# First self attention, units that begin with their scores: all maxima, projections and turned rows behind them

## The chip, the core and the metric

The kernel runs on one core of a Trainium2 chip. The metric is the device time of one execution in microseconds. Before the change it is 1828.26 us (median of 3 runs, 1827.87 to 1830.49).

## The reference

Two decoder blocks work one after the other on x (2 batches, 1024 tokens, width 256). Each has a self attention, a cross attention to 77 context rows, and a feed-forward layer, with a layer norm before each. The change touches only the first block's self attention, with 16 heads of width 64 and no mask:

```
h = _layernorm(x, ln1_g, ln1_b)
q = (xq @ wq).reshape(B, S, N_HEADS, D_HEAD)      # k, v alike
attn = jnp.einsum('bihd,bjhd->bhij', q, k) * scale
attn = jax.nn.softmax(attn, axis=-1)
out = jnp.einsum('bhij,bjhd->bihd', attn, v).reshape(B, S, D_ATTN)
x = out @ wo + bo + x
```

## The kernel before

The function `wide_attention` computes this attention. A **block** is one group g of 2 heads for one batch b; there are 16 (8 groups times 2 batches), written by `both(g, b)`. A block has 8 **units** u0 to u7, and a unit has two **steps**: a step is 128 keys against 512 queries for both heads, steps 0 to 7 for the first half of the queries, 8 to 15 for the second. The groups 1 to 6 run in a loop, the others are written out.

What a unit does on each engine:

- ScalarE writes ("seeds") minus the row maxima into the banks of the scores (L1243), TensorE adds the scores on them (`scores`, L1164: 3 products of high and low parts, 2 heads, so 6 matmuls a step), ScalarE takes the exponential into `sa_p_buf` (L1233), GpSimd adds up the exponentials for the denominators (L1412), TensorE multiplies the exponentials of the unit before with the values (`weighted`, L1179), two steps behind.
- Beside it stand **items** of preparation, for this block ("c"), the next ("n") or the one before ("p"), by the table `lanes`: ("k", h) and ("q", h) project keys and queries (`project`, L1110, 6 matmuls); ScalarE takes the high part out of the bank (L1226) and VectorE the rest (L1307). ("m", qt, half) are maxima: 2 matmuls, one for each head, of 128 queries against 512 keys into two banks (`maxima`, L1126), and VectorE reduces each bank to row maxima (L1325). ("t", h) turns the joined maxima (joined by VectorE at L1340, turned at L1131), VectorE copies them (L1333) and two DMAs take them through memory to all partitions (L1050, L1052). ("den", h) sums the denominators (L1138), ScalarE copies them out (L1256), VectorE inverts them (L1347).

All items share three banks, `sa_front0` to `sa_front2`, used in turn. Which bank each item has and what must have been emptied before is worked out once (`places`), and TensorE waits for it in front of an item (`wait_free`), for both banks of a maxima item before its first matmul. The scores have four banks and the weighted sums the eighth.

The order of work on TensorE is the order in which `both` writes it. `leading` gives the items of a unit up to and with its first maxima item, `trailing` the rest. In front of the scores of a unit stand the leading items, behind them the trailing ones, then the weighted sums. ScalarE, VectorE and GpSimd have their own written orders and meet TensorE at semaphores only. The table for all blocks but the first:

```
0: [("c", ("m", 5, 1)), ("c", ("m", 6, 1)), ("n", ("k", 0))],
1: [("c", ("m", 7, 1)), ("n", ("q", 0)), ("c", ("t", 1)), ("p", ("den", 1))],
2: [("n", ("m", 0, 0)), ("n", ("m", 1, 0)), ("n", ("k", 1))],
3: [("n", ("m", 2, 0)), ("n", ("m", 3, 0))],
4: [("n", ("m", 0, 1)), ("n", ("m", 1, 1)), ("n", ("q", 1))],
5: [("n", ("m", 2, 1)), ("n", ("m", 3, 1)), ("c", ("den", 0))],
6: [("n", ("t", 0)), ("n", ("m", 4, 0)), ("n", ("m", 5, 0))],
7: [("n", ("m", 6, 0)), ("n", ("m", 7, 0)), ("n", ("m", 4, 1))],
```

The first block has a table of its own (`lanes_first`) with the values' projections (L764) added. The last block has no items for a next one.

Of the kernel before, what the change touches and what calls it, by code (L numbers as in the profile page):

```python
# [51 lines left out]
def lin(g, b, per, k):  # L52

    return g * (2 * per) + (b * per + k)
# [762 lines left out]
def wide_attention(nc, name, hT, ident, ones, first_w, oT, spare, prefetch=()):  # L817
# [55 lines left out]
    def lanes_of(g, b):  # L873

        return lanes_first if isinstance(g, int) and (g, b) == (0, 0) else lanes
# [51 lines left out]
    def bank(item, k=0):  # L927
        return BODY[item, k] % NBANK

    def is_first(g, b):  # L930
        return isinstance(g, int) and (g, b) == (0, 0)

    def is_last(g, b):
        return isinstance(g, int) and (g, b) == (NG - 1, 1)
# [5 lines left out]
    def before(g, b):  # L940
        return (g, 0) if b == 1 else (g - 1, 1)
# [4 lines left out]
    def owner(who, g, b):  # L946

        if who == "c":
            return g, b
        if who == "p":  # L950
            return None if is_first(g, b) else before(g, b)
        return None if is_last(g, b) else after(g, b)

    def owned(u, g, b):

        return [(owner(who, g, b), item) for who, item in lanes_of(g, b)[u] if owner(who, g, b) is not None]

    def leading(u, g, b):

        table = lanes_of(g, b)[u]  # L960
        first = [item[0] for _, item in table].index("m") + 1
        return [x for x in owned(u, g, b) if x[1] in [item for _, item in table[:first]]]

    def trailing(u, g, b):

        return owned(u, g, b)[len(leading(u, g, b)):]

    def sums(s):

        return (KT - 1) * (s // KT) + max(s % KT, 1)  # L970
# [12 lines left out]
    with ExitStack() as ctx:  # L983
# [61 lines left out]
        with nc.Block() as block:  # L1045
# [39 lines left out]
            def _(pe):  # L1085
                def wait_free(g, b, item, *made_of):

                    at = 2 * g + b if isinstance(g, int) else 2 + b
                    counts = [DRAINED[at, part, 0] for part in made_of]
                    for k in range(2 if item[0] == "m" else 1):  # L1090
                        by, value = FREE[at, item, k]
                        if by == "den":
                            pe.wait_ge(den_taken, value if isinstance(g, int) else shifted(value, g, HALVES))
                        elif by == "front":
                            counts.append(value)
                    if counts:
                        pe.wait_ge(drained, max(counts) if isinstance(g, int) else shifted(max(counts), g, NDRAIN))

                def project(g, b, item):
                    a = 0 if item[0] == "q" else 1  # L1100
                    fr = front_ps[bank(item)]
                    if item == ("k", 0):
                        pe.wait_ge(w_split, g + 1)
                    c = b * HALVES + item[1]
                    if isinstance(g, int) and g == 0:
                        pe.wait_ge(h_low, c + 1)
                    parts = [(ws[:, a, kd, :], hs[:, kd, tokens(c)]) for kd in range(KD)
                             for ws, hs in ((w_hi, h_hi), (w_hi, h_lo), (w_lo, h_hi))]
                    for n, (ws, hs) in enumerate(parts):
                        mm = pe.matmul(fr[:], ws, hs, start=(n == 0), stop=(n == len(parts) - 1))  # L1110
                    mm.then_inc(front_full, 1)

                def values(n):
                    if n in IN_FRONT:
                        if n >= IN_FRONT.start + NSCORE:
                            pe.wait_ge(v_made, n - NSCORE + 1)
                        first_w.values(pe, n, spare_bank(n)).then_inc(v_full, 1)
                    else:
                        first_w.values(pe, n, front_ps[bank(("v", n))][:]).then_inc(front_full, 1)

                def maxima(g, b, item):
                    _, qt, half = item
                    wait_free(g, b, item, ("q", qt // QH), ("k", half))
                    for j in range(G):
                        r = slice(dh * j, dh * j + dh)
                        pe.matmul(front_ps[bank(item, j)][:], q_hi[r, b, qt * P:(qt + 1) * P],  # L1126
                                  k_hi[r, b, half * HALF:(half + 1) * HALF], start=True, stop=True).then_inc(front_full, 1)

                def turn(g, b, item):
                    pe.wait_ge(joined, lin(g, b, HALVES, item[1] + 1))  # L1130
                    pe.transpose(front_ps[bank(item)][0:G * QH, 0:P], m_row[:].rearrange("p g t -> p (g t)"),  # L1131
                                 ident[:]).then_inc(front_full, 1)

                def denominators(g, b, item):
                    h = item[1]
                    pe.wait_ge(added, lin(g, b, NADD, (KT - 1) * (h + 1)))
                    for j in range(G):
                        mm = pe.matmul(front_ps[bank(item)][64 * j:64 * j + 64, :], ones[:, 0:64], acc[:, h, j, :],  # L1138
                                       start=True, stop=True)
                    mm.then_inc(front_full, 1)  # L1140

                def front_item(g, b, item):
                    if item[0] == "m":
                        maxima(g, b, item)
                        return
                    if not (item[0] == "v" and item[1] in IN_FRONT):
                        wait_free(g, b, item)
                    if item[0] in ("q", "k"):
                        project(g, b, item)
                    elif item[0] == "v":  # L1150
                        values(item[1])
                    elif item[0] == "t":
                        turn(g, b, item)
                    else:
                        denominators(g, b, item)

                def scores(g, b, s):
                    h, kt = divmod(s, KT)
                    pe.wait_ge(seeded, lin(g, b, TILES, (s + 1) * G))
                    keys, queries = slice(kt * P, (kt + 1) * P), slice(h * HALF, (h + 1) * HALF)  # L1160
                    for part, (ks, qs) in enumerate(((k_hi, q_hi), (k_hi, q_lo), (k_lo, q_hi))):
                        for j in range(G):
                            r = slice(dh * j, dh * j + dh)
                            mm = pe.matmul(score_ps[s % len(score_ps)][:, j, :], ks[r, b, keys], qs[r, b, queries], start=False,  # L1164
                                           stop=(part == 2), skip_group_check=True)
                            if part == 2:
                                mm.then_inc(score_full, 1)
# [18 lines left out]

                def both(g, b):
                    for u in range(UNITS):
                        for of, item in leading(u, g, b):
                            front_item(*of, item)  # L1190
                        scores(g, b, 2 * u)
                        scores(g, b, 2 * u + 1)
                        for of, item in trailing(u, g, b):
                            front_item(*of, item)
                        if u >= 1:
                            weighted(g, b, 2 * u - 2)
                            weighted(g, b, 2 * u - 1)
                        elif not is_first(g, b):
                            weighted(*before(g, b), STEPS - 2)
                            weighted(*before(g, b), STEPS - 1)  # L1200
                    if is_last(g, b):
                        weighted(g, b, STEPS - 2)
                        weighted(g, b, STEPS - 1)
                        wait_free(g, b, ("den", 1))
                        pe.wait_ge(added, lin(g, b, NADD, sums(STEPS - 3)))
                        for j in range(G):
                            parts = [acc[:, 1, j, :]] + [p_buf[:, n % NPB, j, :] for n in (STEPS - 2, STEPS - 1)]
                            for n, p in enumerate(parts):
                                mm = pe.matmul(front_ps[bank(("den", 1))][64 * j:64 * j + 64, :], ones[:, 0:64], p,
                                               start=(n == 0), stop=(n == len(parts) - 1))  # L1210
                        mm.then_inc(front_full, 1)
# [1400 lines left out]
```

## Time and profile before

| | |
|---|---|
| median of 3 runs | 1828.26 us |
| profiled execution | 1825.43 us, span 1823.7 us |
| TensorE clock granted, mean | 0.98 |
| matmul busy | 1666.9 us (91%) |
| VectorE, ScalarE, GpSimd busy | 1167.3, 1067.1, 960.0 us |
| scores of the first self attention | from 74.8 to 763.8 us of the span |

The profile records one execution. PE is TensorE's matmuls, PEld its weight loads, DVE VectorE, ACT ScalarE, POOL GpSimd, SPq the queue that issues DMAs. Names starting with sa_ belong to the attention at hand; x and o are buffers lent to it. In a timeline each row is a start, a duration, an engine and what it did; a time in brackets is idle time of the engine before it and what ended it. Ends of matmuls are modelled, so starts are the better guide. In rows of TensorE "x2" are the two heads' matmuls, which start together in the two halves of the array; an fp32 product that is not split into parts is recorded as two.

### The profile page before, as it was taken

Reading aid. Unit: us, or ns where it says so; the run is one execution under the profiler, and the core shown is the slowest. Engines: PE = TensorE matmul, PEld = TensorE weight load, DVE = VectorE, ACT = ScalarE, POOL = GpSimd, SP = SyncE. Lnnn points to the kernel's source line nnn. Section 1 sums busy time; section 2 is a strip of 40 time slices with the busy share of each in tenths; the row PEclk is TensorE's granted clock in tenths of the full one; section 3 lists DMA queues with packets and bytes.
Section 4 is the critical chain, followed back from the end, with each engine's and each line's share of the span. In section 5 each row is a group of like instructions: output and inputs, shape, how many; then the busy total and the mean of one; then the engine's idle time right before and its main releaser. Section 6 shows DMA issues by size and latency. Waiting matters only on the chain. (4 is left out here: it accounts for less than half of the span.)

```text
span 1823.7 us, 28743 instructions
## 1 busy us (share of the span) xinstructions
PE 1666.9 (91%) x9636; PEld 1034.5 (57%) x9636; DVE 1167.3 (64%) x2023; ACT 1067.1 (59%) x1407; POOL 960.0 (53%) x734
## 2 busy tenths in 40 slices
PE   5889999999999999898999889996989988898799
PEld 3334444444444444386666878884544436555679
DVE  4456777767777777375776843447787845787613
ACT  4437888888888888744554433310676773444452
POOL 1237898888889888851222620201334443666205
PEclk9999999999999999999999999996999999999999
DMA  2001211101111111030000011102334321000001
GB/s 90 18 24 35 68 53 35 40 35 43 55 40 35 40 35 48 12 105 26 1 1 1 13 33 26 28 12 66 75 72 106 72 72 31 10 1 7 28 17 47
DMA packets 54210, 70.84 MB, mean 39 GB/s; under 512 B 18208, under 2 KB 41916, under 8 KB 54111
## 3 DMA queue, kind: packets, MB, share of 16 engines
q1 hardware_dynamic: 54111, 69.54, 13.5%
q8 instruction: 59, 0.97, 0.2%
q14 instruction: 40, 0.33, 0.1%
HBM read 41.72 MB, written 2.37 MB: 24 GB/s over the span
## 5 line engine op out<-in xcount | busy, mean ns | idle before, releaser
L1412 POOL TENSOR_TENSOR x<-x,sa_p_buf 128x1024 f32<-128x1024 f32 x190 | 452.5, 2382 | 107.7 <-ACT sa_p_buf L1233 95.3
L1325 DVE TENSOR_REDUCE sa_mx<-sa_front 128x1 f32<-128x512 f32 x512 | 327.3, 681 | 109.2 <-PE sa_front L1126 107.4
L1233 ACT ACTIVATE sa_p_buf<-sa_score 128x1024 f32<-128x1024 f32 x256 | 249.2, 1024 | 116.6 <-PE sa_score L1164 116.6
L1179 PE MATMUL sa_out<-sa_p_buf,sa_v_buf 128*64 128x512 f32 x1024 | 246.2, 602 | 0.0
L607 ACT ACTIVATE sa_p_buf<-sa_score 128x1024 f32<-128x1024 f32 (+1 forms) x160 | 140.6, 942 | 75.0 <-PE sa_score L555 74.8
L402 DVE TENSOR_REDUCE sa_mx<-sa_front 128x1 f32<-128x512 f32 (+1 forms) x224 | 136.5, 651 | 31.3 <-PE sa_front L316 27.6
L1987 POOL TENSOR_TENSOR x<-x,bias_out 128x1024 f32<-128x1024 f32 x24 | 60.1, 2518 | 164.5 <-POOLq L2316 142.0
L1854 POOL TENSOR_TENSOR ca_probs<-ca_s_sb,ca_inv 128x616 f32<-128x616 f32 x64 | 78.1, 1220 | 120.5 <-DVE ca_inv L1770 120.5
L1179 PEld LDWEIGHTS sa_out<-sa_p_buf,sa_v_buf 128*64 128x64 f32 x1024 | 64.9, 136 | 126.8 <-issue 99.1
L1126 PE MATMUL sa_front<-sa_k_hi,sa_q_hi 64*128 64x512 f32 x512 | 116.7, 451 | 19.1 <-DVE sa_mx L1325 15.6
L1243 ACT ACTIVATE sa_score<-sa_m_all 128x1024 f32<-128x1024 f32 x128 | 130.8, 1034 | 0.4 <-ACT o L775 0.4
L1243 ACT ACTIVATE sa_score<-x 128x1024 f32<-128x1024 f32 x128 | 127.6, 1029 | 2.3 <-DMA x<-sa_m_line 2.3
L660 POOL TENSOR_SCALAR_AFFINE_SELECT sa_p_buf<-sa_p_buf 128x128 f32<-128x128 f32 x256 | 66.0, 296 | 119.3 <-ACT sa_p_buf L607 119.3
L1347 DVE RECIPROCAL x<-x 128x128 f32<-128x128 f32 x124 | 108.7, 920 | 17.8 <-ACT x L1256 17.6
L1126 PEld LDWEIGHTS sa_front<-sa_k_hi,sa_q_hi 64*128 64x128 f32 x512 | 48.0, 183 | 124.6 <-DVE sa_mx L1325 61.4
L1164 PE MATMUL sa_score<-sa_q_hi,sa_k_hi 64*128 64x512 f32 x512 | 108.2, 419 | 2.9 <-ACT sa_score L1243 2.9
L1677 ACT ACTIVATE ca_turned<-ca_t_ps 128x1024 f32<-128x1024 f32 x64 | 65.5, 1024 | 73.7 <-PE ca_t_ps L1623 73.7
L1164 PE MATMUL sa_score<-sa_q_hi,sa_k_lo 64*128 64x512 f32 x512 | 101.1, 390 | 0.0
L1164 PE MATMUL sa_score<-sa_q_lo,sa_k_hi 64*128 64x512 f32 x512 | 100.9, 390 | 0.0
L1412 POOL TENSOR_TENSOR x<-sa_p_buf 128x1024 f32<-128x1024 f32 x32 | 76.2, 2382 | 33.9 <-ACT sa_p_buf L1233 33.9
L316 PE MATMUL sa_front<-sa_k_top,sa_q_top 33*128 33x128 f32 (+4 forms) x504 | 71.2, 348 | 22.9 <-DVE sa_mx L402 16.0
L316 PEld LDWEIGHTS sa_front<-sa_k_top,sa_q_top 33*128 33x128 f32 (+1 forms) x504 | 43.7, 193 | 77.1 <-DVE sa_mx L402 51.5
(241 smaller groups left out, 3528.6 us busy)
## 6 DMA issues: line engine op xcount, KB each, us to landing
sa_v_buf<-o SPq DMA_DIRECT2D x16, 512.0 KB, 5.1
sa_m_all<-sa_m_line SPq DMA_DIRECT2D x16, 512.0 KB, 3.7
x<-sa_m_line SPq DMA_DIRECT2D x16, 512.0 KB, 4.3
x<-in_x SPq DMA_DIRECT2D x8, 512.0 KB, 6.8
sa_q_stack<-sa_hi SPq DMA_DIRECT2D x32, 128.0 KB, 2.7
sa_k_stack<-sa_hi SPq DMA_DIRECT2D x32, 128.0 KB, 2.6
sa_recip<-sa_den_out SPq DMA_DIRECT2D x32, 128.0 KB, 2.7
ff_w<-in_L_xattn_ff_w SPq DMA_DIRECT2D x16, 128.0 KB, 2.2
```

The source lines that it names most:

```text
L316: mm = pe.matmul(bank(i, item, u)[:, c0 + lo_k:c0 + hi_k], q_top[base:base + rows_of, b, r, at], k_top[base:base + rows_of, b, r, k0 + lo_ ...
L402: dve.tensor_reduce(mx[:, b, j, place:place + 1], fr[u][:, 0:n], AX.X, ALU.max).then_inc(drained, 1)
L607: nc.scalar.activation(p_buf[:, n % NPB, 2 * r:2 * r + 2, 0:cols], score_ps[r][:, :, 0:cols], ACT.Exp, scale=SCALE).then_inc(exp_done, 1)
L1126: pe.matmul(front_ps[bank(item, j)][:], q_hi[r, b, qt * P:(qt + 1) * P], k_hi[r, b, half * HALF:(half + 1) * HALF], start=True, stop=True) ...
L1164: mm = pe.matmul(score_ps[s % len(score_ps)][:, j, :], ks[r, b, keys], qs[r, b, queries], start=False, stop=(part == 2), skip_group_check= ...
L1179: mm = pe.matmul(out_ps[64 * j:64 * j + 64, :], v_buf[:, b, kt, 64 * j:64 * j + 64], p_buf[:, s % NPB, j, :], start=(kt == 0), stop=(kt == ...
L1233: nc.scalar.activation(p_buf[:, s % NPB], score_ps[s % len(score_ps)][:], ACT.Exp, scale=SCALE).then_inc(exp_done, G)
L1243: nc.scalar.activation(score_ps[s % len(score_ps)][:], m_all[h].rearrange("p (j n) -> p j n", j=G), ACT.Identity).then_inc(seeded, G)
L1325: dve.tensor_reduce(mx[:, b, j, qt, half:half + 1], front_ps[bank(item, j)][:], AX.X, ALU.max).then_inc(drained, 1)
L1347: dve.reciprocal(recip[:, h, at], recip[:, h, at]).then_inc(inverted, 1)
L1412: nc.gpsimd.tensor_tensor(acc[:, h], prev, cur, ALU.add).then_inc(added, 1)
L1854: nc.gpsimd.tensor_tensor(probs[:, n % 2, :, 0:TC], s_sb[:, n % NS], inv[:, n % 2, :].unsqueeze(2).to_broadcast((P, U, TC)), ALU.mult).the ...
```

## The change

`leading` and `trailing` are gone. In each unit TensorE now has the scores of both steps first, and then all items of the unit in the table's order, and the weighted sums. Tables, banks, the counts waited for and the other engines' programs are as they were.

```
                 def both(g, b):
                     for u in range(UNITS):
-                        for of, item in leading(u, g, b):
-                            front_item(*of, item)
                         scores(g, b, 2 * u)
                         scores(g, b, 2 * u + 1)
-                        for of, item in trailing(u, g, b):
+                        for of, item in owned(u, g, b):
                             front_item(*of, item)
                         if u >= 1:
                             weighted(g, b, 2 * u - 2)
```

The first place is u3 of a block on TensorE. sa0_front is a bank of the items, sa0_score0 and sa0_score1 are the scores of the unit's two steps. Before:

```order
L1126 MATMUL sa0_front0<-sa0_k_hi,sa0_q_hi 128x512
L1126 MATMUL sa0_front1<-sa0_k_hi,sa0_q_hi 128x512
L1164 MATMUL sa0_score0<-sa0_q_hi,sa0_k_hi 128x512 x2
L1164 MATMUL sa0_score0<-sa0_q_lo,sa0_k_hi 128x512 x2
L1164 MATMUL sa0_score0<-sa0_q_hi,sa0_k_lo 128x512 x2
L1164 MATMUL sa0_score1<-sa0_q_hi,sa0_k_hi 128x512 x2
L1164 MATMUL sa0_score1<-sa0_q_lo,sa0_k_hi 128x512 x2
L1164 MATMUL sa0_score1<-sa0_q_hi,sa0_k_lo 128x512 x2
L1126 MATMUL sa0_front2<-sa0_k_hi,sa0_q_hi 128x512
L1126 MATMUL sa0_front0<-sa0_k_hi,sa0_q_hi 128x512
L1179 MATMUL sa0_out<-sa0_p_buf,sa0_v_buf 64x512 x4
```

The same unit now (the lines' numbers are lower by ten):

```order
L1154 MATMUL sa0_score0<-sa0_q_hi,sa0_k_hi 128x512 x2
L1154 MATMUL sa0_score0<-sa0_q_lo,sa0_k_hi 128x512 x2
L1154 MATMUL sa0_score0<-sa0_q_hi,sa0_k_lo 128x512 x2
L1154 MATMUL sa0_score1<-sa0_q_hi,sa0_k_hi 128x512 x2
L1154 MATMUL sa0_score1<-sa0_q_lo,sa0_k_hi 128x512 x2
L1154 MATMUL sa0_score1<-sa0_q_hi,sa0_k_lo 128x512 x2
L1116 MATMUL sa0_front0<-sa0_k_hi,sa0_q_hi 128x512
L1116 MATMUL sa0_front1<-sa0_k_hi,sa0_q_hi 128x512
L1116 MATMUL sa0_front2<-sa0_k_hi,sa0_q_hi 128x512
L1116 MATMUL sa0_front0<-sa0_k_hi,sa0_q_hi 128x512
L1169 MATMUL sa0_out<-sa0_p_buf,sa0_v_buf 64x512 x4
```

The six rows of scores moved ahead of the first maxima item, so the second item's use of bank 0 stands two matmuls behind the first one's.

The second place is u6 on TensorE, which has the turned row (L1131 before, L1121 now). Before:

```order
L1131 MATMUL sa0_front2<-ident,sa0_m_row 8x128
L1126 MATMUL sa0_front0<-sa0_k_hi,sa0_q_hi 128x512
L1126 MATMUL sa0_front1<-sa0_k_hi,sa0_q_hi 128x512
L1164 MATMUL sa0_score0<-sa0_q_hi,sa0_k_hi 128x512 x2
...
L1164 MATMUL sa0_score1<-sa0_q_hi,sa0_k_lo 128x512 x2
L1126 MATMUL sa0_front2<-sa0_k_hi,sa0_q_hi 128x512
L1126 MATMUL sa0_front0<-sa0_k_hi,sa0_q_hi 128x512
```

And now:

```order
L1154 MATMUL sa0_score0<-sa0_q_hi,sa0_k_hi 128x512 x2
...
L1154 MATMUL sa0_score1<-sa0_q_hi,sa0_k_lo 128x512 x2
L1121 MATMUL sa0_front2<-ident,sa0_m_row 8x128
L1116 MATMUL sa0_front0<-sa0_k_hi,sa0_q_hi 128x512
L1116 MATMUL sa0_front1<-sa0_k_hi,sa0_q_hi 128x512
L1116 MATMUL sa0_front2<-sa0_k_hi,sa0_q_hi 128x512
L1116 MATMUL sa0_front0<-sa0_k_hi,sa0_q_hi 128x512
```

The turned row moved behind the scores with the maxima that led.

## Rows read from the trace of the kernel before

**Rows 1.** Busy time by stretch: PE, PEld, DVE, ACT, POOL, granted clock, DMA
```profile
300.00:400.00 100.00, 97.66 (x545) 47.62 (x544) 74.80 (x119) 85.69 (x100) 88.22 (x42) 1.00 0.12 40
...
100.00:130.00 30.00, 25.75 (x110) 11.49 (x109) 14.99 (x26) 11.88 (x14) 10.42 (x5) 1.00 0.11 36
...
776.00:780.00 4.00, 4.00 (x10) 3.19 (x10) 2.36 (x2) 4.00 (x4) 0.00 (x0) 0.50 0.71 231
```
**Rows 2.** Timeline of TensorE, u0 and the start of u1
```profile
400.50 0.50 PE L1126 MATMUL sa_front<-sa_k_hi,sa_q_hi 64*128 64x512 f32 x2
...
400.84 0.40 PE L1164 MATMUL sa_score<-sa_q_hi,sa_k_hi 64*128 64x512 f32 x2
...
402.22 0.39 PE L1126 MATMUL sa_front<-sa_k_hi,sa_q_hi 64*128 64x512 f32 x2
402.54 0.50 PE L1110 MATMUL sa_front<-sa_h_hi,sa_w_hi 128*128 128x512 f32 x1
...
404.14 1.94 PE L1179 MATMUL sa_out<-sa_p_buf,sa_v_buf 128*64 128x512 f32 x8
406.01 0.50 PE L1126 MATMUL sa_front<-sa_k_hi,sa_q_hi 64*128 64x512 f32 x2
...
407.83 0.51 PE L1110 MATMUL sa_front<-sa_h_hi,sa_w_hi 128*128 128x512 f32 x1
```
**Rows 3.** Timeline of VectorE in u0 and u1
```profile
401.04 1.29 DVE L1325 TENSOR_REDUCE sa_mx<-sa_front 128x1 f32<-128x512 f32 x2 [1.01 <-PE sa_front L1126]
402.64 1.29 DVE L1325 TENSOR_REDUCE sa_mx<-sa_front 128x1 f32<-128x512 f32 x2 [0.32 <-PE sa_front L1126]
...
407.87 0.17 DVE L1340 TENSOR_REDUCE sa_m_row<-sa_mx 128x8 f32<-128x16 f32 x1
```
**Rows 4.** Timeline of TensorE, u7 to the next block
```profile
436.40 0.51 PE L1126 MATMUL sa_front<-sa_k_hi,sa_q_hi 64*128 64x512 f32 x2
...
438.47 0.40 PE L1126 MATMUL sa_front<-sa_k_hi,sa_q_hi 64*128 64x512 f32 x2
439.64 0.50 PE L1126 MATMUL sa_front<-sa_k_hi,sa_q_hi 64*128 64x512 f32 x2 [0.78 <-DVE sa_mx L1325]
440.07 1.94 PE L1179 MATMUL sa_out<-sa_p_buf,sa_v_buf 128*64 128x512 f32 x8
441.94 0.50 PE L1126 MATMUL sa_front<-sa_k_hi,sa_q_hi 64*128 64x512 f32 x2
```
**Rows 5.** Timeline of TensorE, first block
```profile
83.66 0.40 PE L1126 MATMUL sa_front<-sa_k_hi,sa_q_hi 64*128 64x512 f32 x2
85.42 0.50 PE L1110 MATMUL sa_front<-sa_h_hi,sa_w_hi 128*128 128x512 f32 x1 [1.37 <-DVE sa_mx L1325]
...
115.30 0.49 PE L1126 MATMUL sa_front<-sa_k_hi,sa_q_hi 64*128 64x512 f32 x2 [0.78 <-DVE sa_mx L1325]
117.17 0.50 PE L1110 MATMUL sa_front<-sa_h_hi,sa_w_hi 128*128 128x512 f32 x1 [1.38 <-DVE sa_mx L1325]
```
**Rows 6.** Timeline of TensorE, u4 and the start of u6
```profile
421.65 0.49 PE L1126 MATMUL sa_front<-sa_k_hi,sa_q_hi 64*128 64x512 f32 x2
...
424.04 0.50 PE L1110 MATMUL sa_front<-sa_h_hi,sa_w_hi 128*128 128x512 f32 x1
...
432.29 0.27 PE L1131 MATMUL sa_front<-ident,sa_m_row 128*8 128x128 f32 x1
```
**Rows 7.** Timeline of ScalarE, u0
```profile
401.83 1.94 ACT L1233 ACTIVATE sa_p_buf<-sa_score 128x1024 f32<-128x1024 f32 x2 [1.41 <-PE sa_score L1164]
...
403.65 1.03 ACT L1243 ACTIVATE sa_score<-sa_m_all 128x1024 f32<-128x1024 f32 x1
```
**Rows 8.** DMA queue, its landing (KB, us), and the seed that needs it
```profile
434.55 0.33 SPq L1052 DMA_DIRECT2D sa_m_all<-sa_m_line  x1
...
sa_m_all<-sa_m_line SPq DMA_DIRECT2D x1, 512.0 KB, 3.9
...
439.70 1.02 ACT L1243 ACTIVATE sa_score<-sa_m_all 128x1024 f32<-128x1024 f32 x1
```

More of the change, by code:

```diff
@@ L956, in owned @@
         return [(owner(who, g, b), item) for who, item in lanes_of(g, b)[u] if owner(who, g, b) is not None]
[L958 to L966, printed above, removed]
     def sums(s):
@@ L1188, in both @@
                     for u in range(UNITS):
-                        for of, item in leading(u, g, b):
-                            front_item(*of, item)
                         scores(g, b, 2 * u)
                         scores(g, b, 2 * u + 1)
-                        for of, item in trailing(u, g, b):
+                        for of, item in owned(u, g, b):
                             front_item(*of, item)
```

## The prediction

> **What bounds the kernel now.** I read the busy time by stretch first: in the first self attention TensorE is 98% busy at full clock, GpSimd 88%, ScalarE 86%, VectorE 75% [rows 1]. A busy share does not say that an engine has no holes, so I then read the timeline of one block (one group of heads of one batch; eight units u0 to u7) on TensorE. The reader is to look at the start times, not at the durations: two matmuls of one kind in the two halves of the array start as a pair, and the six pairs of a unit's scores take 402.22 - 400.84 = 1.38, 0.23 each, though each is recorded as 0.39. By start times a unit is maxima 0.34, scores 1.38, maxima 0.32, projection 1.60, weighted sums 1.87, and then the next unit's maxima, with nothing left between [rows 2]. So TensorE's program order is the path here. A block takes 441.94 - 400.50 = 41.44 us [rows 2, 4]; the first exponential after the scores starts 401.83 - 400.84 = 0.99 after them, and the seed that the next unit's scores need starts 1.82 later and takes 1.03 [rows 7], so scores could follow scores after some 3.9 us, and all units but the short ones take longer. ScalarE is ahead.
>
> Next come the three banks that maxima, projections, turned rows and sums share. One maxima item fills two of them, VectorE empties both in 1.29, and starts 0.54 after the matmuls when they come first after other work, 0.42 when matmuls of the same kind ran before [rows 2, 3]. Two maxima items need four banks. The scores between them hide this: 400.50 to 402.22 is 1.72, longer than the 1.29 in which the first bank is free again (0.54 + 0.75, see next). Where two items stand together, the second waits: 438.47 to 439.64 is 1.17, which is 0.42 and 0.75 for the first of the two reductions and the signal behind it [rows 4]. A projection behind two maxima waits for both banks: 83.66 to 85.42 is 1.76, and behind an item that itself had waited 115.30 to 117.17, 1.87 [rows 5]. These three prices are the whole prediction.
>
> **The change, part by part.** No instruction is added or removed, and only TensorE's order changes. In a full block the leading maxima go behind the scores in all units, and so the turned row in u6. ScalarE, VectorE, GpSimd and the DMA queue keep their orders. What waits behind a stalled maxima item on TensorE is the projection, the weighted sums and, through them, the next unit's scores; ScalarE's exponentials and GpSimd's additions wait for those.
>
> I sum from the start of a unit to the start of its last part (weighted sums, or the projection or sums before it), which keep their own length. Scores that come straight behind the weighted sums pay the slow first pair that the maxima paid (0.34 for 0.23): 1.38 + 0.11 = 1.49.
>
> u0, u2 and u5 (two maxima, then a projection or the sums in the bank that the first item's second matmul used): before 402.54 - 400.50 = 2.04. After 1.49 + 1.76 = 3.25. +1.21 each, 3.63.
> u3 (two maxima, then the weighted sums, which need no such bank): after 1.49 + 1.17 + 0.43 (439.64 to 440.07) = 3.09. +1.05.
> u4 (as u0): before 424.04 - 421.65 = 2.39 [rows 6], 0.35 more than in u0, because in a short unit's wake its scores wait for seeds; after it 3.25, since the longer u3 gives ScalarE the time. +0.86.
> u7 (three maxima): before 440.07 - 436.40 = 3.67, after 1.49 + 1.17 + (0.54 + 0.75 = 1.29) + 0.43 = 4.38. +0.71.
> u6 (turned row and two maxima): before 436.40 - 432.29 less 1.87 of weighted sums = 2.24, after 1.49, a change of kind 0.10, the turned row 0.20 (2.24 - 2.04), then 1.29 + 0.43 = 3.51. +1.27. The trace has no turned row behind scores; its cost lies between nothing (its 0.20 is paid in both) and a wait of 0.5 for VectorE's copy of it; I take the 0.10.
> u1 (one maxima item, projection, turned row): maxima and scores change places at no cost, 1.82 before [rows 2] and 1.49 + 0.32 after. But the turned row waits for the joined maxima. They stood ready 407.87 + 0.17 = 408.04 [rows 3], over a microsecond before their use; now VectorE begins at 1.91 and ends at 3.20, joins to 3.41, and the turned row, due at about 3.3, goes at 3.5. +0.25.
>
> A full block: 3.63 + 1.05 + 0.86 + 0.71 + 1.27 + 0.25 = 7.77 us, and 14 such blocks are 109 us. The first block has the same items and the values beside them, so its banks already wait: by the same steps seven units lose 0.3 to 1.4 and one gains 0.6 (its scores need no longer wait for the maxima's bank), +7. The last has maxima in two units only; u0 is like u3 (+1.05), and u1 has no projection in front of its turned row, which so waits in full: 3.5 instead of 2.04 (+1.5). The units behind have no maxima and stay as they are: +2.6. Sum 109 + 7 + 2.6 = 118.6, say 118. The profiled execution took 1825.4 (span 1823.7), so 1943.5; the median shown is 2.8 above it, so the prediction is 1946. Nothing behind this attention changes.
>
> What hides nothing: VectorE has the room (a block grows by a fifth, its work does not), and its reciprocals stand behind the maxima, so they delay none. Nothing is gained from earlier exponentials, since TensorE never waits for one.
>
> **Bounds of what the trace does not show.** From below: if only the first kind of wait came in full (0.94 above the pace of 0.23, in seven units) and the further 0.6 (projection, turned row, third maxima) and the 0.5 in u1 and u6 did not, a block loses 6.6 and the sum is 92 + 8, 1928. From above: if each restart cost another 0.11 and the late projections pushed the second seed past the second half of the scores by 0.15, a block loses 9.8, the sum is 137 + 12, 1977. A gain is excluded by rows 4 and 5 unless the rival below holds. I take the middle sum, which is nearest to the rows.
>
> **The rivals.** (a) The waits are hidden and the kernel gets faster. For it: ScalarE, GpSimd and VectorE have 14%, 12% and 25% idle, earlier scores start exponentials 0.34 sooner, and the seed waits of u4 and u7 (0.35 each) go: 14 x 0.7 = 10 us less, 1818. It decides if the second maxima can follow the first within about 0.3 us; rows 4 and 5 show 1.17 at all places where they stand together. Weight loads fill only 48% of TensorE's time [rows 1]. The Trainium skill (Perfetto Trace Analysis, Identifying the Most-Contended Engine) says that matmul occupancy misleads and that the weight loads' share is to be read; read so, TensorE has half its time free, which would speak for this rival, while the trace's start times leave no such room.
>
> (b) The rows of maxima come late. Turned row to landed broadcast takes 434.55 + 3.9 - 432.29 = 6.2, and the first seed of the next block starts 7.4 after the turned row, so 1.2 is spare [rows 6, 8]. In the new order the turned row comes 1.8 after the scores of u6, lands at 8.0 and is wanted at 5.4 + 2.8 = 8.2 (u6's length, then exponentials in u7): 0.2 spare by these figures. Against it: VectorE was busy when it came and will be free now, some 0.3 more. If it missed by 1 to 2 us in each block, 14 to 28 us come on top: 1960 to 1974.
>
> (c) The clock falls. In the first block, where waits of this sort already stand, TensorE was granted 1.00; where it came back from a real pause it got 0.50, that is the lower of 1.2 and 2.4 GHz [rows 1]. If one block in ten ran at the lower level, it would take about 41 us more, in all some 60: 2005. The Trainium skill (TensorE: Matmul & The Clock Gate, A second HAM failure mode: psum-queue depth-cycling) describes just this, an engine that idles briefly between groups of matmuls while it cycles through PSUM banks and whose clock then swings; by that rule the time would be this rival's. The trace does not agree: 1.00 from 100 to 130 us with waits of 0.8 to 1.4 us.
>
> **How the numbers follow.** The forecast's mechanism near its size 0.80 (its own range 1932 to 1962); the same mechanism at its lower bound 0.06; (b) 0.07; (c) 0.04; (a) 0.03. The range takes in the lower bound and half of the way to the upper one: 1926 to 1966. Slower 0.96, the same 0.01, faster 0.03; a change of this kernel within 0.2% cannot be told from none.
>
> **What would show it.** A block of about 49.2 us instead of 41.4; TensorE's idle before its maxima, which VectorE's maxima end, well over 80 us instead of a few; gaps of 1.17 between the pairs of maxima in all units but u1 and 1.76 from the first of them to the projection; ScalarE and GpSimd with the same busy time and more waits; clock 1.00; hardly any seed waits in front of scores. Wrong would be: blocks under 48 or over 51 us, waits for seeds or for the row of maxima in front of scores, or a clock under 1.

## The result and the profile after

The changed kernel takes 1978.43 us (median of 4 runs, 1976.29 to 1979.75); before, in runs beside it, 1829.38 us (4 runs). The ratio is 1.0811, with a 95% interval of 1.0788 to 1.0834: 8.1% slower. The forecast was slower, at 1946, with a range to 1966; the time lies 12 us above the range. The profiled execution took 1978.45 us with a span of 1976.7, 153.0 more than the span before; the forecast had 118 of them.

Busy time by stretch of the changed kernel, with the columns of [rows 1] (PE, PEld, DVE, ACT, POOL, granted clock, DMA):

```profile
300.00:400.00 100.00, 86.44 (x444) 40.52 (x442) 60.80 (x95) 68.78 (x80) 71.82 (x33) 0.97 0.10 34
...
100.00:115.00 15.00, 13.28 (x41) 5.61 (x42) 6.54 (x12) 2.47 (x3) 4.36 (x2) 0.85 0.15 37
...
470.00:472.00 2.00, 2.00 (x8) 0.39 (x4) 0.36 (x1) 0.00 (x0) 2.00 (x2) 0.50 0.00 0
```

All four engines are less busy than in [rows 1], since the same work is spread over more time. The reader should stop at the clock: 0.97 where it was 1.00, and 0.50 in a stretch of 2 us.

The timeline of TensorE in u3, the unit with two maxima items and nothing else:

```profile
441.17 0.50 PE L1154 MATMUL sa_score<-sa_q_hi,sa_k_hi 64*128 64x512 f32 x2
...
442.66 0.39 PE L1116 MATMUL sa_front<-sa_k_hi,sa_q_hi 64*128 64x512 f32 x2
443.84 0.50 PE L1116 MATMUL sa_front<-sa_k_hi,sa_q_hi 64*128 64x512 f32 x2 [0.78 <-DVE sa_mx L1313]
444.27 1.94 PE L1169 MATMUL sa_out<-sa_p_buf,sa_v_buf 128*64 128x512 f32 x8
```

442.66 - 441.17 is 1.49, 443.84 - 442.66 is 1.18, 444.27 - 443.84 is 0.43: the forecast for this unit had 1.49, 1.17 and 0.43. And the same engine from u7 into the next block's u0:

```profile
466.08 0.39 PE L1116 MATMUL sa_front<-sa_k_hi,sa_q_hi 64*128 64x512 f32 x2
467.25 0.49 PE L1116 MATMUL sa_front<-sa_k_hi,sa_q_hi 64*128 64x512 f32 x2 [0.78 <-DVE sa_mx L1313]
468.53 0.51 PE L1116 MATMUL sa_front<-sa_k_hi,sa_q_hi 64*128 64x512 f32 x2 [0.78 <-DVE sa_mx L1313]
468.96 2.96 PE L1169 MATMUL sa_out<-sa_p_buf,sa_v_buf 128*64 128x512 f32 x8
471.85 0.79 PE L1154 MATMUL sa_score<-sa_q_hi,sa_k_hi 64*128 64x512 f32 x2
472.45 0.63 PE L1154 MATMUL sa_score<-sa_q_lo,sa_k_hi 64*128 64x512 f32 x2
472.87 0.52 PE L1154 MATMUL sa_score<-sa_q_hi,sa_k_lo 64*128 64x512 f32 x2
...
473.93 0.39 PE L1116 MATMUL sa_front<-sa_k_hi,sa_q_hi 64*128 64x512 f32 x2
```

The two waits stand where they were forecast, 1.17 and 1.28 behind the item before. Then the weighted sums take 471.85 - 468.96 = 2.89 instead of the 1.87 of [rows 2], and the scores 473.93 - 471.85 = 2.08 instead of 1.49. Nothing waits there; the first pair of the scores is recorded at 0.79 instead of 0.50. This is the stretch granted 0.50, the lower of 1.2 and 2.4 GHz, and it costs 1.02 + 0.59 = 1.61 us. Read in windows of 1 us, the trace has one such fall to 0.50 behind the u7 of each block from the second on, 14 in all, and three more in the first block, from 97, 124 and 138 us.

By the starts of their scores, u0 to u7 take 7.37, 6.40, 6.74, 4.97, 6.71, 6.12, 5.62 and 7.26 us; a block goes from 420.66 to 471.85, which is 51.19, where it took 41.44. The waits of TensorE by what ended them, from 74 us to the end of the attention, after:

```profile
PE sa_front L1116 <- DVE sa_mx L1313: 96.8, 123, 1.4
PE sa_front L1100 <- DVE sa_mx L1313: 5.6, 15, 1.4
...
PE sa_score L1154 <- ACT sa_score L1231: 3.4, 5, 2.1
```

and before:

```profile
PE sa_front L1126 <- DVE sa_mx L1325: 12.5, 16, 0.8
...
PE sa_score L1164 <- ACT sa_score L1243: 2.9, 5, 1.7
```

The columns are the idle time in total, how often, and the longest. Waits in front of maxima for VectorE's maxima went from 16 to 123, about one more in each unit but u1, which is what the change does.

### The profile page after: what moved, and what is told of

The parts are those of the page before. It is cut to its first block and busy times, and to the rows that moved or that the text cites. A ratio compares the mean times of both kernels' runs of the same rounds, so it can differ in the third digit from the quotient of the medians.

```text
span 1976.7 us, 28743 instructions
## 1 busy us (share of the span) xinstructions
PE 1727.3 (87%) x9636; PEld 1046.6 (53%) x9636; DVE 1174.4 (59%) x2023; ACT 1072.3 (54%) x1407; POOL 956.5 (48%) x734
## 5 line engine op out<-in xcount | busy, mean ns | idle before, releaser
L1169 PE MATMUL sa_out<-sa_p_buf,sa_v_buf 128*64 128x512 f32 x1024 | 260.8, 632 | 0.0
L402 DVE TENSOR_REDUCE sa_mx<-sa_front 128x1 f32<-128x512 f32 (+1 forms) x224 | 136.5, 651 | 31.4 <-PE sa_front L316 27.9
L1154 PE MATMUL sa_score<-sa_q_hi,sa_k_hi 64*128 64x512 f32 x512 | 120.7, 468 | 3.5 <-ACT sa_score L1231 3.4
L1154 PEld LDWEIGHTS sa_score<-sa_q_hi,sa_k_hi 64*128 64x128 f32 x512 | 50.9, 195 | 133.1 <-ACT sa_score L1231 100.2
```

Of the source, the lines that this page charges most:

```text
L402: dve.tensor_reduce(mx[:, b, j, place:place + 1], fr[u][:, 0:n], AX.X, ALU.max).then_inc(drained, 1)
L1169: mm = pe.matmul(out_ps[64 * j:64 * j + 64, :], v_buf[:, b, kt, 64 * j:64 * j + 64], p_buf[:, s % NPB, j, :], start=(kt == 0), stop=(kt == ...
```

## The experiments

Each kernel is one of the two with an edit, which is shown; the ratios are to runs of the kernel before on the same chips (medians 1828.2 to 1830.3).

**e1_lead_u7: the lead restored in u7 alone.**

```
+ahead = leading(u, g, b) if u == 7 else []
+for of, item in ahead:
+    front_item(*of, item)
 scores(g, b, 2 * u)
 scores(g, b, 2 * u + 1)
-for of, item in owned(u, g, b):
+for of, item in owned(u, g, b)[len(ahead):]:
     front_item(*of, item)
```

> The changed order, but in u7 (the unit with three maxima items) the first item leads the scores again. The changed kernel's block is 51.2 us where the sum gave 49.2, and in its trace TensorE's granted clock is 0.50 for some 3.4 us behind u7. Theory C (the waits of u7 stand so close together that the clock falls there, and nowhere else): u7 gives back its 0.71 us of waits and the whole dip, 1.7 us a block, so 14 to 15 blocks give 34 us: about 1944, clock 1.00 through the attention, block about 48.8. Rival L (the missing 2 us are longer signals, restarts or seeds in all units, the clock is a by-product): only u7's waits go, 14 x 0.7 = 10 us: about 1968, block 50.5.

Measured: 1945.09 us, ratio 1.0629 (1.0593 to 1.0664). One unit of eight gives back 33.3 of the 149 us, 2.3 in each of 14.5 blocks, though its waits are worth 0.71. The stretch's row:

```profile
400.00:500.00 100.00, 87.19 (x461) 41.05 (x461) 63.10 (x100) 73.19 (x85) 74.42 (x34) 1.00 0.11 34
```

TensorE has as many holes as in the changed kernel (87% busy), and its clock is 1.00. It is 1.00 from 145 to 700 us; in the first block it still falls (0.86 from 74 to 145 us), which theory C had not expected. So theory C holds for the full blocks: there the slow stretch hangs on u7.

**e2_only_u7: the order of before, u7 alone begins with its scores.** The condition above is `u != 7`.

> The order of before, but u7 alone begins with its scores, all three maxima behind them. Theory C local (the dip needs only u7's two waits and the scores and sums around them): +0.71 of waits, -0.35 of seed wait, and 1.7 of slow clock in each of 15 blocks: 1829 + 15 x 2.1 = about 1860, clock 0.50 behind u7. Rival C long (the dip needs the waits of the units before u7 as well): 1829 + 15 x 0.4 = about 1835, clock 1.00.

Measured: 1864.48 us (1858.10 to 1872.48), ratio 1.0179 (1.0130 to 1.0228), and the profiled execution had a span of 1870.8. The timeline and the windows behind u7:

```profile
462.56 0.58 PE L1126 MATMUL sa_front<-sa_k_hi,sa_q_hi 64*128 64x512 f32 x2 [0.78 <-DVE sa_mx L1326]
463.07 1.97 PE L1179 MATMUL sa_out<-sa_p_buf,sa_v_buf 128*64 128x512 f32 x4
...
466.50 0.50 PE L1126 MATMUL sa_front<-sa_k_hi,sa_q_hi 64*128 64x512 f32 x2
```

```profile
463.00:466.00 3.00, 3.00 (x10) 0.76 (x8) 1.39 (x3) 0.31 (x1) 2.92 (x2) 0.50 0.00 0
466.00:470.00 4.00, 4.00 (x24) 2.48 (x22) 2.58 (x4) 2.18 (x3) 1.62 (x3) 0.97 0.00 0
```

The weighted sums take 466.50 - 463.07 = 3.43 instead of 1.87. The row x4 is cut off by the window; all eight matmuls of the sums lie between 463.07 and 466.50. The two waits of one unit suffice (the row shows the second, the first ends at 461.29); the waits of the other seven are not needed. The runs of this kernel scatter more than others' (14 us between the ends). Two runs took 1858.1 and 1858.2 us at a mean granted clock of 0.972, two took 1870.8 and 1872.5 at 0.965; time multiplied by clock is 1805 to 1807 in all four, so the difference is the clock. The profiled run, the slowest, has the fall behind every u7. At 1.56 us a fall (3.43 - 1.87) the faster two had, by an estimate, some nine falls fewer; by that estimate the same two waits do not bring the clock down every time.

**e3_only_u3: the order of before, u3 alone begins with its scores.** The condition is `u != 3`.

> The order of before, but u3 alone (two maxima and nothing else) begins with its scores. Theory B (the second item waits for VectorE's reduction of the first): u3 +1.05 us, and u4's 0.35 us wait for seeds goes because ScalarE got the time: +0.70 a block, 15 blocks, 1829 + 10 = about 1839; the two pairs of maxima stand 1.17 apart in u3. Rival (the seeds give nothing back): 1829 + 16 = 1845. Rival hidden (a wait in one unit is taken up by others): 1829 to 1832.

Measured: 1842.38 us, ratio 1.0076 (1.0054 to 1.0099): 14 us or 0.9 to 1.0 a block, between the 0.70 of the sum with the seed wait given back and the 1.05 without; the interval (10 to 18 us) excludes neither. The timeline of u3 and u4 shows the wait and the missing seed wait both:

```profile
469.09 0.40 PE L1126 MATMUL sa_front<-sa_k_hi,sa_q_hi 64*128 64x512 f32 x2
470.26 0.50 PE L1126 MATMUL sa_front<-sa_k_hi,sa_q_hi 64*128 64x512 f32 x2 [0.78 <-DVE sa_mx L1326]
...
472.56 0.50 PE L1126 MATMUL sa_front<-sa_k_hi,sa_q_hi 64*128 64x512 f32 x2
...
474.36 0.50 PE L1126 MATMUL sa_front<-sa_k_hi,sa_q_hi 64*128 64x512 f32 x2
474.95 0.50 PE L1110 MATMUL sa_front<-sa_h_hi,sa_w_hi 128*128 128x512 f32 x1
```

u4 takes 474.95 - 472.56 = 2.39 to its projection, as in [rows 6], although its scores no longer wait for seeds: its second maxima item now starts 0.08 later than in u0 of [rows 2] and its projection a further 0.27 later, behind VectorE, whose reciprocals of u3 (1.75 us) stand between the later maxima of u3 and those of u4. So in this order u3's delay is not given back. In the changed kernel it is, since there u4 is late itself.

**e4_sums_between: scores first, the weighted sums behind the first maxima item, in all units.**

```
 scores(g, b, 2 * u)
 scores(g, b, 2 * u + 1)
-for of, item in owned(u, g, b):
+for of, item in leading(u, g, b):
     front_item(*of, item)
 (weighted sums of two steps)
+for of, item in trailing(u, g, b):
+    front_item(*of, item)
```

> Each unit begins with its scores as in the changed kernel, but the weighted sums stand between the first maxima item and the rest, so that VectorE empties the banks under 1.7 us of other matmuls. Theory B (only the neighbourhood of maxima costs, beginning with the scores costs nothing): waits in front of maxima are those of before (u7 alone), one more change of kind in the units with a projection (about 0.2 each, 4 units), seed waits gone: 1829 plus 0 to 12 us, about 1835, clock 1.00. Rival (scores ahead of the maxima cost by themselves, through later rows of maxima or later exponentials): over 1870.

Measured: 1946.61 us, ratio 1.0645 (1.0609 to 1.0681). A miss by 110 us, and near the rival, but not for its reason. The waits in front of maxima are gone where they should be; others came. A unit with a projection:

```profile
459.34 0.40 PE L1110 MATMUL sa_front<-sa_h_hi,sa_w_lo 128*128 128x512 f32 x1
459.67 0.50 PE L1164 MATMUL sa_score<-sa_q_hi,sa_k_hi 64*128 64x512 f32 x2
459.77 0.60 ACT L1226 ACTIVATE sa_k_hi<-sa_front 128x512 fp32r<-128x512 f32 x1 [2.13 <-PE sa_front L1110]
460.27 1.02 ACT L1243 ACTIVATE sa_score<-sa_m_all 128x1024 f32<-128x1024 f32 x1
...
461.34 0.50 PE L1164 MATMUL sa_score<-sa_q_hi,sa_k_hi 64*128 64x512 f32 x2 [0.71 <-ACT sa_score L1243]
```

ScalarE stands 2.13 us idle in front of its copy of the projection, since the projection now is the last thing of a unit; the seed of the second step is written behind that copy, and so the second half of the next scores waits 0.71. Where the sums of the denominators are last, ScalarE's copy of them stands in front of both seeds, and the scores wait 1.70. The weighted sums had covered these two copies. I had priced the moved sums by what they cover on VectorE and not asked what they had covered on ScalarE. The clock was not 1.00 either: it fell to 0.50 from 245, 344, 443 and 689 us, each time 1.0 to 1.4 us behind the end of the one wait of 1.70 that a block has. In most blocks the same wait brought no fall.

**e8_sums_between_u367: the same only in u3, u6 and u7**, which have neither at their end.

> The changed kernel, but in u3, u6 and u7, which have no projection and no sums of denominators behind their maxima, the weighted sums stand behind the first maxima item. The kernel with the sums between in all units took 1946.6 us, and its trace has waits of 0.7 and 1.7 us for seeds where a projection or the denominators stand at the end of a unit. Theory S (those waits come from ScalarE, whose next seed stands behind the copy of the projection or of the denominators): here no such copy is late, so u3 and u6 lose 0.9 of waits each, u7 0.9 and the slow clock 1.7: 14.5 x 4.4 = 64 us, about 1915. Rival (sums between maxima cost by themselves, through more changes of kind or late sums): 1950 or more.

Measured: 1941.34 us, ratio 1.0616 (1.0584 to 1.0648): 37 us less than the changed kernel, where 64 were expected. The waits for seeds of e4 are gone, so that reading stands, but a new one came:

```profile
526.94 1.29 DVE L1326 TENSOR_REDUCE sa_mx<-sa_front 128x1 f32<-128x512 f32 x2 [1.01 <-PE sa_front L1126]
...
528.14 1.75 DVE L1348 RECIPROCAL x<-x 128x128 f32<-128x128 f32 x2
...
528.46 0.40 PE L1126 MATMUL sa_front<-sa_k_hi,sa_q_hi 64*128 64x512 f32 x2
...
529.82 1.22 DVE L1326 TENSOR_REDUCE sa_mx<-sa_front 128x1 f32<-128x512 f32 x2
...
530.50 0.49 PE L1126 MATMUL sa_front<-sa_k_hi,sa_q_hi 64*128 64x512 f32 x2 [1.64 <-DVE sa_mx L1326]
```

In u4 the second maxima item starts 530.50 - 528.46 = 2.04 behind the first, not 1.17: VectorE's two reciprocals of u3 stand behind the maxima that came late in u3, and in front of u4's. That is 0.87 a block or 13 us of the missing 27; the clock, 0.98 in two of the five stretches of 100 us between 200 and 700 us, is another part, some 2 falls. Both follow the wait of 1.64 in a u4 (they begin at 242.4 and 580.3); in the other blocks the same wait brought none. The rest I did not follow.

**e5_half_reduce: the changed kernel, VectorE reduces 256 of the 512 columns.**

```
-dve.tensor_reduce(mx[...], front_ps[bank(item, j)][:], AX.X,
+dve.tensor_reduce(mx[...], front_ps[bank(item, j)][:, 0:HALF // 2], AX.X,
```

> The changed kernel, but VectorE reduces only the first 256 of the 512 columns of each maxima bank (so the maxima leave out half of the keys), which takes some 0.4 instead of 0.69 us. Nothing of TensorE's work or order changes. Theory B (the waits are VectorE's reductions): second maxima 0.90 behind the first instead of 1.17, projection 1.33 instead of 1.76; a block loses 3.0 us of waits, and with them the slow clock (1.7): 14.5 x 4.7 = 68 us, about 1910; if the clock still falls, 1935. Rival (the wait is made by TensorE's own restart and signals, not by the length of the reduction): 1970 to 1978.

Measured: 1903.38 us, ratio 1.0404 (1.0368 to 1.0440). Its maxima and its clock:

```profile
454.44 0.39 PE L1116 MATMUL sa_front<-sa_k_hi,sa_q_hi 64*128 64x512 f32 x2
454.86 0.42 DVE L1313 TENSOR_REDUCE sa_mx<-sa_front 128x1 f32<-128x256 f32 x1 [2.30 <-PE sa_front L1116]
455.34 0.49 PE L1116 MATMUL sa_front<-sa_k_hi,sa_q_hi 64*128 64x512 f32 x2 [0.51 <-DVE sa_mx L1313]
```

```profile
400.00:500.00 100.00, 91.26 (x490) 43.83 (x490) 48.32 (x103) 75.25 (x87) 78.18 (x36) 1.00 0.14 45
```

The second item stands 0.90 behind the first, as expected: 0.42 to the reduction's start, 0.42 for it, 0.06 for the signal. TensorE's program is untouched, so the waits are the length of VectorE's reductions, and with them shorter the slow stretch behind u7 is gone too (1.00 from 145 to 700 us; two falls are left in the first block).

**e7_between_scores: the first maxima item between the scores of the two steps.**

```
 scores(g, b, 2 * u)
+for of, item in leading(u, g, b):
+    front_item(*of, item)
 scores(g, b, 2 * u + 1)
```

> Each unit begins with the scores of its first step only, then the leading items, the second step's scores, and the rest. So 0.7 us of matmuls stand between the first two maxima, where before has 1.4 and the changed kernel none. Theory B: second maxima still 1.17 behind the first, 0.25 of it as a wait, projection 1.76 behind the first: u0, u2, u4, u5 +0.2 to 0.5 over before, u3 +0.35, u7 as before: some 3 us a block, about 1870, clock 1.00. Rival (any wait between maxima costs about the full amount, through restarts or the clock): over 1930. Rival (0.7 us suffice): 1830.

Measured: 1872.02 us, ratio 1.0231 (1.0200 to 1.0262). With 1.4, 0.7 and no microseconds of scores between the first two maxima, the kernel takes 1829, 1872 and 1978. The price goes with how much of the 1.17 is uncovered; of the 1978, some 14 x 1.61 = 23 are the clock, which e7 keeps at 1.00 in the full blocks.

**e6_two_a_unit: the order of before, the third maxima item of u7 moved to u1 of the next block.**

```
-1: [("c", ("m", 7, 1)), ("n", ("q", 0)), ("c", ("t", 1)), ("p", ("den", 1))],
+1: [("c", ("m", 4, 1)), ("c", ("m", 7, 1)), ("n", ("q", 0)), ("c", ("t", 1)), ("p", ("den", 1))],
-7: [("n", ("m", 6, 0)), ("n", ("m", 7, 0)), ("n", ("m", 4, 1))],
+7: [("n", ("m", 6, 0)), ("n", ("m", 7, 0))],
```

> The order of before with one entry of the table moved: the third maxima item of u7 (the row that next block needs last) goes to u1, which had one, so no unit has more than two and scores stand between any two. Theory B: the one wait of before in front of maxima (0.85 a block) goes; u1 gets one more item (0.23, which u7 loses) and its turned row may wait 0.1 to 0.2 for the joined maxima: -0.65 a block, 15 blocks: about 1819, faster than both. Rival (u7's wait was covered by ScalarE's pace in the units behind it, where scores wait for seeds): 1826 to 1830.

Measured: 1818.89 us (10 runs), ratio to before 0.9950 (0.9934 to 0.9966): faster than both kernels. Its u7:

```profile
472.06 0.51 PE L1126 MATMUL sa_front<-sa_k_hi,sa_q_hi 64*128 64x512 f32 x2
...
474.12 0.40 PE L1126 MATMUL sa_front<-sa_k_hi,sa_q_hi 64*128 64x512 f32 x2
474.45 1.94 PE L1179 MATMUL sa_out<-sa_p_buf,sa_v_buf 128*64 128x512 f32 x8
476.32 0.51 PE L1126 MATMUL sa_front<-sa_k_hi,sa_q_hi 64*128 64x512 f32 x2
```

The wait of [rows 4] is not there any more.

This trace holds one thing more. Its first block has the same program as before, and the place of [rows 5] comes with the same two waits, 0.78 and 1.38 us. Here is the place, with the clock behind it, and then the clock behind the same place in the kernel before:

```profile
113.61 0.49 PE L1126 MATMUL sa_front<-sa_k_hi,sa_q_hi 64*128 64x512 f32 x2 [0.78 <-DVE sa_mx L1325]
115.48 0.57 PE L1110 MATMUL sa_front<-sa_h_hi,sa_w_hi 128*128 128x512 f32 x1 [1.38 <-DVE sa_mx L1325]
115.85 0.63 PE L1110 MATMUL sa_front<-sa_h_lo,sa_w_hi 128*128 128x512 f32 x1
```

```profile
116.00:118.00 2.00, 2.00 (x7) 1.52 (x6) 0.00 (x0) 0.00 (x0) 0.43 (x1) 0.50 0.00 0
```

```profile
117.00:122.00 5.00, 4.83 (x14) 2.57 (x14) 1.50 (x3) 1.52 (x2) 1.13 (x1) 1.00 0.00 0
```

The same work with the same waits was granted 0.50 in one execution and 1.00 in the other.

**e9_scores_first_two_a_unit: the changed kernel with the same two lines of the table changed.**

> The changed kernel with the table entry of the two-a-unit experiment: the third maxima item of u7 stands in u1. Every unit still begins with its scores, and every unit but none has two maxima side by side with the full wait. Theory C (the clock falls only where two waits stand close behind each other, with u7's three items): clock 1.00 through the attention; u7 loses 1.29 of the third item and 1.7 of slow clock, u1 gains a second item with its wait, 1.2 to 1.5: 1.5 to 1.8 a block less, about 1954. Rival (the clock falls once a block from the sum of the waits, wherever they stand): the slow stretch is still there, behind another unit: 1975 to 1985.

Measured: 1955.61 us (1953.18 to 1967.55), ratio 1.0702 (1.0658 to 1.0746), 23 us less than the changed kernel, 21 to 25 expected (20 if the ratios are compared). The clock of the profiled execution:

```profile
400.00:500.00 100.00, 86.20 (x459) 40.72 (x459) 61.45 (x96) 71.68 (x82) 72.49 (x33) 1.00 0.10 34
```

TensorE is 86% busy, no more than in the changed kernel (86.5% in that stretch), and has as many maxima items that wait; only no unit has two waits of 0.78 in a row (a wait of 0.18 in front of a projection does follow one). The clock stays at 1.00 from 145 to 700 us; in the first block it falls twice. So it is not the sum of the holes alone that brings the clock down here; where they stand counts. It is no certain rule: the slowest of the four runs took 1967.55 us at a mean clock of 0.970, the others 1953 to 1956 at 0.976 to 0.979.

## Why the prediction was wrong

**Right: direction, mechanism and the waits.** The rows showed TensorE's order as the path, and two maxima items side by side as a wait of 1.17 [rows 4] with a projection 1.76 behind [rows 5]. After the change u2, u3 and u4 take 6.74, 4.97 and 6.71 by the starts of their scores; the sum had 3.25 + 1.60 + 1.87 = 6.72 for a unit with a projection and 3.09 + 1.87 = 4.96 for u3. u1 took 6.40, where its 6.23 of before (412.24 - 406.01) and the forecast 0.25 make 6.48. Half the reduction (e5) and half the cover (e7) changed the time by about what the same terms gave, 1903 for 1910 and 1872 for 1870.

**Wrong: the clock, which the forecast took as 1.00 with a chance of 0.96.** The step that failed is the dismissal of rival (c): "The trace does not agree: 1.00 from 100 to 130 us with waits of 0.8 to 1.4 us." So the sum had the clock at nothing. The dismissal was too much for what it rested on: one execution, in which the 0.78 and 1.38 in a row of [rows 5] went by at 1.00. In the trace of e6 the same two waits at the same place were followed by 0.50, so the one trace could not exclude the fall. It also had no place with two waits in a row in front of the weighted sums, as u7 was to get. In the trace after, the slow stretch follows u7 and costs 1.61, 14 x 1.61 = 23 of the 35 us that the forecast lacks in the span (153 against 118); e1 and e9 take it away in the full blocks, e2 makes it alone. Rival (c) itself had the place wrong too: it took one block in ten at half clock throughout, and it was a few microseconds in each block. Two of the signs that the prediction itself called wrong came: a block over 51 us and a clock under 1. The Trainium skill (TensorE: Matmul & The Clock Gate, A second HAM failure mode: psum-queue depth-cycling) describes a clock that swings when TensorE idles briefly between groups of matmuls while it goes through PSUM banks; with u7's three items this trace agrees, at 0.50 and 1.61 us a block, while e9, with as many waits spread out, held 1.00 from 145 to 700 us of the profiled execution.

**The sum, set right.** The block grew by 51.19 - 41.44 = 9.75 where 7.77 were forecast. Of the 1.98, 1.61 are the clock; the other 0.37 are in u5 and u6, which took 6.12 and 5.62 where the sum had 5.98 and 5.38. In u6 the second half of the scores still waits for a seed: it starts 0.94 behind the first half instead of 0.80, and after that restart its first pair is slow again, so that the turned row starts 0.90 behind it where the sum had 0.79. "Hardly any seed waits" was thus too strong. Fourteen blocks give 136.5 us. The first block grew by 13.4 instead of 7: its scores start at 74.6 and u1 of the next block at 172.10, against 74.8 and 157.66, a difference of 14.7, of which 1.2 belong to the next block's u0. Its granted clock, 0.85 between 100 and 115 us and 0.89 between 115 and 145, is a part of the further 6 us. Its three falls add up to some 13.6 us at 0.50, which can cost 6.8 at most and so could be all of it; how much of it they are was not tested. From the start of its u0 to its last weighted sums the last block took 916.11 - 881.18 = 34.93, before 763.79 - 732.01 = 31.78: 3.15 more, of which 0.6 is the end of the last slow stretch, so its 2.6 came as forecast. Together 136.5 + 13.4 + 3.1 = 153.

**The rivals.** (a) is refuted: no unit got shorter, and e7 shows the price rising with the uncovered time. (b) did not come: the turned row at 460.81, the broadcast issued at 462.65 and landed 3.8 later at 466.45, the seed at 467.51, so 1.1 us were spare, not 0.2. The row landed 0.56 earlier than the 6.2 of the forecast, mostly because VectorE copied the turned row at once (2.26 us from turned row to broadcast before, 1.84 now), and the seed came 0.3 later than forecast.

**The bounds.** The range's upper end was built from restarts and seeds (1977, a block 9.8 longer) and then cut to 1966. That 1977 and 9.8 are almost what was measured is chance: of the 1.98 a block above the middle sum, restarts and seeds were 0.37 and the clock 1.61. No bound contained the clock, although a rival with a price of 60 us did. A rival that could come in part, not only as a whole, belonged into the range.

## What to carry to other kernels

Where an engine's written order puts other work between two uses of a small pool of banks, price a reordering by the time from a use to its release (here 1.17) less what stays between; the rows at any place where two uses already stand together give that price. Ask the same of each block of work that is moved: on every engine, what did it cover, and what stands in line there (e4 and e8 both failed on this). When the new order puts several waits close together on TensorE, price the lower clock for the matmuls behind them as a part of the range, also where one trace of the old order shows such waits at 1.00, since another execution may not (e6); and if one place of the old order already shows such a wait, moving one item may be worth more than the change at hand (e6, 0.5% faster).

## What the runs showed of the hardware

In the changed kernel the granted clock fell to 0.50 although TensorE had idled only twice for 0.78 us: before it fell the engine had run 1.5 us of scores and then three pairs of maxima, 1.17 and 1.28 apart. The clock is 1.00 up to 469 us and 0.50 from 470 to 473 us, so it fell within the weighted sums that start at 468.96; these and the first scores behind them ran slow, though nothing made them wait, and from 473.24 on the pairs are 0.23 apart again. With the same two waits in a kernel that is otherwise 96% busy (e2) it fell too, behind every u7 of the profiled execution. With waits in nearly every unit, but never two of 0.78 in a row, and 86% busy (e9) it was 1.00 from 145 to 700 us of the profiled execution. In the kernel before, with one such wait in u7, it is 1.00 from 100 to 700 us.

Two waits in a row are not the only thing that was followed by a fall. In e4 a block has one wait of 1.62 to 1.70, and four of these 14 were followed by a fall; in e8 it has one of 1.61 to 1.64 in u4, and two were. And the same place was granted 1.00 in one execution and 0.50 in another (before and e6, behind waits of 0.78 and 1.38). What decides between them no run here shows.
